# Two scalings of the softmax probabilities moved from ScalarE to VectorE, behind the reciprocal

## The reference

```
logits  = einsum('bqhk,bthk->bhqt', qh, kh) / sqrt(K)      # kh: 256 keys and one bias key
weights = softmax(logits, axis=-1)
ctx     = einsum('bhqt,bthk->bqhk', weights, vh)
```

## Time and profile before

| what | value |
|---|---|
| three runs | 2339.66, 2343.88, 2346.64 us (median 2343.88) |
| the profiled execution | 2339.65 us, span 2337.8 us |
| PE busy | 2281.9 us, 98% of the span |
| PEld busy | 1989.4 us, 85% |
| DVE busy | 1411.3 us, 60% |
| POOL busy | 1250.0 us, 53% |
| ACT busy | 1165.5 us, 50% |
| chain that ended last | PE 87%, ACT 5%, DVE 4%, POOL 1% |
| ACT's scalings L1221 | 512 instructions, 230.0 us |
| DVE's reciprocals L1525 | 256 instructions, 41.5 us |

### The profile page before, as it was taken

One profiled execution on the slowest core, in us unless ns is written; L12 is line 12 of the kernel. 1 busy time (PEld: TensorE's weight loads), 2 busy tenths in 40 slices (PEclk: granted clock), 3 DMA queues, 4 the chain that ended last, 5 costly groups with the idle time before them and its releaser, 6 DMA issues.

```text
span 2337.8 us, 36326 instructions
## 1 busy us (share of the span) xinstructions
PE 2281.9 (98%) x13192; PEld 1989.4 (85%) x13192; DVE 1411.3 (60%) x2380; ACT 1165.5 (50%) x2967; POOL 1250.0 (53%) x983
## 2 busy tenths in 40 slices
PE   7999998999999999999999989999999998999999
PEld 5899997899997888888888878888888887788887
DVE  4666666666665666666666776666666666534433
ACT  3323232322224766666666767666666666422222
POOL 3877772887757674344443775644435545611110
PEclk9999999999999999999999999999999999999999
DMA  4454543354544222222222212222222220100001
GB/s 170 145 190 163 190 163 118 127 198 156 194 159 137 72 73 73 69 73 73 66 79 65 73 55 64 73 78 64 76 70 80 75 64 19 36 28 28 27 1 72
DMA packets 83439, 218.33 MB, mean 93 GB/s; under 512 B 9536, under 2 KB 12096, under 8 KB 83264
## 3 DMA queue, kind: packets, MB, share of 16 engines
q1 hardware_dynamic: 82544, 215.91, 27.5%
q10 hardware_dynamic: 720, 0.10, 0.0%
HBM read 144.41 MB, written 71.57 MB: 92 GB/s over the span
## 4 chain that ended last, share of the span: by engine, by line
PE 87%; ACT 5%; DVE 4%; POOL 1%; issue 1%; DMA 1%; SPq 0%; DVEq 0%; ACTq 0%
PE U L842 22%; PE U L844 22%; PE U L843 22%; PE T L987 4%; PE O L842 2%; PE S L844 2%; PE O L844 2%; PE O L843 2%; PE S L843 2%; PE S L842 2%; DVE hT L1494 1%; ACT probs L1221 1%; ACT aff L1180 1%; PE S L1029 1%; ACT probs L1213 1%
## 5 line engine op out<-in xcount | busy, mean ns | idle before, releaser
L1513 DVE TENSOR_TENSOR x<-x,U 128x512 f32<-128x512 f32 x384 | 261.1, 683 | 80.8 <-PE U L844 78.5
L1213 ACT ACTIVATE probs<-S,nm 128x257 f32<-128x257 f32 x512 | 238.2, 477 | 35.8 <-DVE nm L1521 35.8
L1521 DVE TENSOR_REDUCE nm<-S 128x2 f32<-128x514 f32 x256 | 177.3, 692 | 123.1 <-PE S L844 119.3
L1231 ACT ACTIVATE PT<-T 128x512 fp32r<-128x512 f32 x256 | 152.6, 596 | 173.4 <-PE T L987 172.4
L1221 ACT ACTIVATE probs<-probs,rs 128x256 f32<-128x256 f32 x512 | 230.0, 499 | 0.5 <-DVE rs L1525 0.5
L842 PE MATMUL U<-wos,oT 128*128 128x512 f32 x512 | 213.5, 417 | 0.2 <-DVE gT L1504 0.2
L1536 DVE SCALAR_TENSOR_TENSOR oT<-O,hc,oT 128x256 fp32r<-128x256 f32 x256 | 123.8, 484 | 144.0 <-ACT oT L1237 144.0
L739 POOL CAST vb<-vb 128x1024 fp32r<-128x1024 f32 x64 | 68.0, 1063 | 262.4 <-DMA vb<-vd 262.4
L844 PE MATMUL U<-wos,oT 128*128 128x512 f32 x512 | 202.0, 395 | 0.0
L843 PE MATMUL U<-wos,oT 128*128 128x512 f32 x512 | 201.2, 393 | 0.0
L1529 DVE TENSOR_TENSOR PT<-T,PT 128x512 fp32r<-128x512 f32 x256 | 175.5, 686 | 42.0 <-ACT PT L1231 42.0
(11 more groups left out here) (246 smaller groups left out, 7242.3 us busy)
## 6 DMA issues: line engine op xcount, KB each, us to landing
kd<-stage SPq DMA_DIRECT2D x128, 258.0 KB, 2.5
kb<-kd SPq DMA_DIRECT2D x64, 516.0 KB, 3.4
vd<-stage SPq DMA_DIRECT2D x128, 256.0 KB, 2.1
vb<-vd SPq DMA_DIRECT2D x64, 512.0 KB, 3.8
raw<-wk SPq DMA_DIRECT2D x32, 512.0 KB, 5.3
rawv<-wv SPq DMA_DIRECT2D x28, 512.0 KB, 4.5
raw<-wa SPq DMA_DIRECT2D x24, 512.0 KB, 4.6
raw<-wb SPq DMA_DIRECT2D x24, 512.0 KB, 5.0
```

The source lines that it names most:

```text
L1213: ins = act.activation(probs[:, r, qt, 0:257], S[:, qt, 0:257], ACT.Exp, bias=nm[:, r, qt:qt + 1], scale=-1.0, accum_out=sums[:, r, qt:qt ...
L1231: act.activation(PT[:, J % 2, 0, :], T[:], ACT.Copy).then_inc(pt_hi, 1)
L1513: dve.tensor_tensor(x[:, tile, :], x[:, tile, :], bank(what, s, t), ALU.add).then_inc(free, 1)
L1521: dve.tensor_reduce(nm[:, J % 2, :], S[:, :, 0:257], AX.X, ALU.min).then_inc(least, 1)
```

## The change

ACT's function `divided` is deleted, and with it its call in every slot and ahead of the slots. DVE's `inverted` is renamed `divided`. Behind the reciprocal, DVE now waits for its own semaphore `inverse` and then does the two multiplications of 128x256, each a tensor_scalar in place with the reciprocal as a scalar for each partition. The second raises `prob`. Nothing else moves: the place of the reciprocal in DVE's list stays, and PE, POOL and SP have the same lists as before.

```
-            def divided(J):
-                r = J % 2
-                act.wait_ge(inverse, J + 1)
-                for qt in range(2):
-                    ins = act.activation(probs[:, r, qt, 0:256], probs[:, r, qt, 0:256], ACT.Copy, scale=rs[:, r, qt:qt + 1])
-                ins.then_inc(prob, 1)
...
                 if J:
                     weighted_hi(J - 1)
-                if J + 1 < ITEMS:
-                    divided(J + 1)
...
-            def inverted(J):
+            def divided(J):
+                r = J % 2
                 dve.wait_ge(exped, J + 1)
-                dve.reciprocal(rs[:, J % 2, :], sums[:, J % 2, :]).then_inc(inverse, 1)
+                dve.reciprocal(rs[:, r, :], sums[:, r, :]).then_inc(inverse, 1)
+                dve.wait_ge(inverse, J + 1)
+                for qt in range(2):
+                    ins = dve.tensor_scalar(probs[:, r, qt, 0:256], probs[:, r, qt, 0:256], rs[:, r, qt:qt + 1], None, ALU.mult)
+                ins.then_inc(prob, 1)
...
                 if J + 1 < ITEMS:
-                    inverted(J + 1)
+                    divided(J + 1)
```

More of the change, by code:

```diff
@@ L1257, in _ @@
                     exponentials(0)
-                elif what == "X":
-                    divided(0)
                 elif what in TO_A:
@@ L1568, in _ @@
                 elif what == "X":
-                    inverted(0)
+                    divided(0)
                 elif what in ("pg", "wy"):
```

## The result

| | median us | runs |
|---|---|---|
| before | 2343.53 | 4, 2339.66 to 2346.64 |
| after | 2460.15 | 4, 2459.03 to 2462.21 |

The ratio is 1.0503, with a 95% interval of 1.0487 to 1.0518. The change makes the kernel 5% slower, by 117 us. The forecast was 2450 us with a range of 2385 to 2485, so the measured time lies 10 us above the forecast and inside the range.

The account below looks back on a forecast made before the run. PE was taken to bound the kernel outside norm. Collisions of 57 + 50 + 14 us less 12 us in norm stages gave 109 us on the profiled 2339.65 us, 2449 us; forecast 2450 us, range 2385 to 2485.

Parts of the forecast that it names:

- What bounds it: Outside norm PE is busy throughout, so relieving ACT gains nothing there and whatever makes PE wait is paid in full.
- Price of a scaling: On DVE, 0.34 us each and 0.59 us a pair; an undisturbed item is ready 0.65 us behind its reciprocal.
- The wait for POOL and the turns: DVE's scalings cannot run beside POOL's casts or subtractions; the engines alternate, so a 2.4 us subtraction can split a pair.
- First collision: Third item, 42 stages with c = 1 to 3: scalings meet POOL's value cast and subtraction, 1.35 us each, 57 us.
- Second collision: Fourth item, 36 of those 42 stages: delayed scalings meet POOL's split of the next keys, 1.4 us each, 50 us.
- Third collision: First item of the 14 stages with c = 1: second scaling waits for POOL's weight subtraction, 1.0 us each, 14 us.
- Norm stages: Eight stages where PE has some 23 us of idle time; half was expected back from relieving ACT, -12 us.
- (a): Rival: only the first waits are real, second collisions cost little; 2403 us, down to 2380; chance 0.24.
- (b): Rival: scalings never wait for POOL, norm stages give 12 to 23 us; 2321 to 2332 us; chance 0.10.
- Rival (c): PE's new gaps, two of 1.4 us a stage, lower the granted clock more often; 2460 to 2480 us; chance 0.08.

Follow-up runs that it names:

- third item only: The kernel before, with only the scalings of each stage's third item (J % 4 == 2) moved to DVE, the others left on ACT: 2402.9 us, ratio 1.0264.
- accumulator form: The changed kernel, but each scaling on DVE also writes the sum of its output, which nothing reads: 2320.82 us, ratio to before 0.9914.

## Why the prediction was right

Time from a stage's first turn to the next stage's first turn in us, by their starts in the traces. A delay of the first item of a stage with c = 1 therefore shows in the column c = 0.

| | c = 0 | c = 1 to 3 | norm: 30, 31, 32, 33 |
|---|---|---|---|
| before | 18.5 to 18.6 | 18.5 to 18.6, two 18.9 | 23.2, 24.1, 26.3, 23.7 |
| after | 19.5 to 19.6 | mostly 21.2 to 21.5 | 23.4, 23.8, 23.1, 23.9 |
| third item only | 18.5 to 18.6 | mostly 19.7 to 20.0 | 24.8, 24.4, 23.6, 23.7 |
| accumulator form | 18.5 to 18.6 | 18.5 to 18.6 | 20.6, 21.2, 22.8, 22.6 |

- **What bounds it.** Right. PE had no idle time outside norm, and 123 us came on top of the 1204.7 us between the first turn of stage 0 and that of stage 63, all of them outside norm (124, against 121 forecast there).
- **Price of a scaling.** Estimated 0.34 us, measured 0.354 in the median. An undisturbed pair ends 0.65 us behind the reciprocal, as worked out.
- **The wait for POOL and the turns.** Right, and shown by three experiments: another form of the instruction, another moment of POOL's work, one scaling instead of two.
- **First collision.** 1.3 us for item 106, measured 1.2. As a sum 57 us; with the third items alone moved, 60 us in the stages where it was placed.
- **Second collision.** 1.5 us for item 107, measured 1.6 from turn to turn. PE waits for the fourth item in 34 of the 42 stages, against 36 counted. As a sum 50 us; the stages of c = 1 to 3 take 109 us more than before with all items moved and 60 with the third alone, so 50 is what the fourth adds. Such a stage was forecast at some 21 us and mostly takes 21.2 to 21.5, in 9 of 42 less.
- **Third collision.** 1.0 us in 14 stages, measured 1.0 to 1.1 in each. Alone it cost more in 6 stages, for the reason shown above. That all 14 fell on the cheap side here was luck in part: the margin read from the earlier trace rows was 0.07 us, and the prediction gave no reason why it would hold.
- **Norm stages.** The term that was mis-sized: -12 us in the sum, measured -0.9 us over seven of the eight (166.1 us before, 165.2 after). There too POOL casts and subtracts beside DVE, and I charged nothing for it: 18 scalings were held by one. In the accumulator form the same seven take 150.9 us, so the relief was worth 15 us and the collisions took nearly all of it; with POOL's work moved by two waits they take 155.2. So this term was 11 us too low in a time 10 us above the forecast; the stages outside norm added 3 us more than forecast, and the last part was 2 us shorter than before. That half of the bound of 23 us would come back was a guess, without a row for it.
- **The other rivals.** (a) fell with the 34 waits for the fourth item, and (b) with the 190 held scalings. What (b) describes is what the form with the accumulator output does: 478 ns, beside POOL, and 20 us faster than before.
- **Signs that were off.** PE was to be busy near 87% outside norm and was busy 91% (436.64 of 480 us). Stages of c = 0 were to take 18.5 us and take 19.5, only because the interval ends behind the third collision. POOL's subtractions were to get longer by 0.1 to 0.3 us, but their mean stayed (L741 2401 against 2402 ns, L733 2422 against 2439).
- **The clock.** Rival (c) fell: the granted clock of the profiled execution was 0.995 over the span, against 0.997 before, and 1.00 outside norm in both.
- **Beside POOL's tensor_scalar.** The sum has no term for it, and the pair of the earlier trace rows was called undisturbed. For the scalings that was not exact: 8 of those of the kernel after were held there, by 0.1 to 0.5 us. Two places in the kernel after, DVE and POOL:

```profile
1376.57 0.97 DVE L1518 TENSOR_SCALAR probs<-probs,rs 128x256 f32<-128x256 f32 x2
...
1375.30 8.29 POOL L760 TENSOR_SCALAR z<-x,mv,rstd 128x512 f32<-128x512 f32 x4 [0.18 <-PE U L844]
...
1429.23 0.97 DVE L1518 TENSOR_SCALAR probs<-probs,rs 128x256 f32<-128x256 f32 x2
...
1426.97 4.13 POOL L760 TENSOR_SCALAR z<-x,mv,rstd 128x512 f32<-128x512 f32 x2
```

Pairs of 0.97 instead of 0.62 us: one of the two scalings waits 0.35 us. POOL's instruction takes 2.08 us, and a scaling that falls on its middle is not held at all: those that started 0.7 to 1.3 us into it took 0.34 to 0.36 us. The two scalings at 1429.23 start 0.2 and 0.8 us into the POOL instruction that ends at 1431.10. They end at 1429.93 and 1430.20, before it does, while each of the 190 scalings that started under a cast or subtraction ended behind it.

## What to carry to other kernels

Before an element-wise step goes from ScalarE to VectorE, look at what GpSimd does at that moment: if it has a form that waits, as this tensor_scalar between SBUF tiles did (up to 2.58 us instead of 0.354), price it by the longest cast or subtraction of GpSimd beside it (2.4 us here) and not by its own duration, and count a pair as two meetings (2.74 and 3.35 us instead of 0.62 for items 106 and 107). Not every step waits: the low part of oT (L1536), which reads the PSUM tile O, took 483 to 486 ns between 820 and 1300 us of the kernel before, with a cast or subtraction of GpSimd beside it or without. Against the changed kernel the form with an accumulator output (478 instead of 354 ns) was worth 6%, and two waits on GpSimd were worth 5%. Against the kernel before, only the first was a gain, of 0.9%. A short delay in one place can move a step onto work whose start was fixed earlier, so follow each delay to the next meeting before summing.

## What the runs showed of the hardware

- The multiplication 128x256 in SBUF takes 354 ns, and 478 ns with the accumulator output, plus a read of some 80 ns that runs beside the next one. The first form waited for POOL's casts and subtractions: in the kernel after all 190 that started under one ended behind it, and the longest of the 512 took 2.58 us. The second never did in 512 instructions, 223 of them beside one, and took 473 to 482 ns.
- A scaling held for long by a cast or subtraction ended 0.14 to 0.16 us behind it. In the kernel after, 107 of the 256 pairs were split: POOL's next instruction was ready and went ahead of DVE's second scaling.
- The starts in the rows do not settle who goes first: in all the kernels with plain scalings, casts and subtractions that started up to 45 ns behind the scaling still won, and those that started 48 ns or more behind it lost.
- A tensor_scalar of POOL over 512 columns (2.08 us) held a scaling near its beginning and near its end, and not in between. In the kernel after, scalings that started 0.2 us into it ended 0.9 us into it, those that started at 0.7 to 1.3 us took 0.34 to 0.36 us, and those from 1.4 to 1.7 us waited for its end. Why, no run shows.
